# Column tiles for a decoder stage's products, maxima rows sent by GpSimd, and a narrow causal mask

## The reference

```
x = _layernorm(x + _L0_attn_ref(...))    # a0: 8 heads of 32, band of +-64 keys, then a GELU FFN
x = _layernorm(x + _L0_xattn_ref(...))   # x0: 16 heads of 16, keys from ctx, causal mask
x = _layernorm(x + _L0_ffn_ref(...))     # FFN with LoRA experts
x = _layernorm(x + _L1_attn_ref(...))    # a1: 16 heads of 16, full attention
x = _layernorm(x + _L1_xattn_ref(...))   # x1: 16 heads of 16, keys from ctx, full with key mask
x = _layernorm(x + _L1_ffn_ref(...))     # top 2 of 8 experts
```

## Time and profile before

| | us |
|---|---|
| median of 3 runs (lowest, highest) | 3195.89 (3194.34, 3197.38) |
| the profiled execution | 3194.37 |
| its span | 3192.6 |
| mean granted TensorE clock | 0.937 of 2.4 GHz |

### The profile page before, as it was taken

One profiled execution on the slowest core, in us unless ns is written; L12 is line 12 of the kernel. 1 busy time (PEld: TensorE's weight loads), 2 busy tenths in 40 slices (PEclk: granted clock), 3 DMA queues, 4 the chain that ended last, 5 costly groups with the idle time before them and its releaser, 6 DMA issues. The chain is left out here.

```text
span 3192.6 us, 83730 instructions
## 1 busy us (share of the span) xinstructions
PE 2810.0 (88%) x34974; PEld 1425.7 (45%) x34975; DVE 2065.5 (65%) x4240; ACT 1568.0 (49%) x2122; POOL 223.8 (7%) x295
## 2 busy tenths in 40 slices
PE   6686987999996997799999999999999999379992
PEld 3474552444544563144434343443433343246661
DVE  3345137888845236688999898988898985312224
ACT  2222322666662322266777776776776768023331
POOL 2001201000000002300000000000000000210003
PEclk9888997999997999699999999999999999589996
DMA  5412033011001004312112212111111110710012
GB/s 155 119 43 94 1 91 91 3 39 39 3 2 37 1 0 126 88 41 64 45 43 51 60 34 55 44 44 54 43 45 44 44 44 2 257 45 31 31 33 87
DMA packets 112871, 173.46 MB, mean 54 GB/s; under 512 B 17882, under 2 KB 88427, under 8 KB 112147
## 3 DMA queue, kind: packets, MB, share of 16 engines
q1 hardware_dynamic: 109460, 160.11, 17.4%
q0 software_dynamic: 3072, 8.39, 0.8%
HBM read 127.63 MB, written 40.51 MB: 53 GB/s over the span
## 5 line engine op out<-in xcount | busy, mean ns | idle before, releaser
L1304 DVE TENSOR_REDUCE d_part_max<-d_ps_m 128x1 f32<-128x512 f32 (+1 forms) x1964 | 1128.0, 631 | 93.5 <-PE d_ps_m L1291 57.0
L1612 ACT ACTIVATE d_prob<-d_ps_s 128x1024 f32<-128x1024 f32 x928 | 898.8, 1021 | 347.8 <-PE d_ps_s L1481 341.0
L1291 PE MATMUL d_ps_m<-k_st,q_st 97*32 97x512 bf16 (+1 forms) x5296 | 482.0, 363 | 19.4 <-DVE d_part_max L1304 15.9
L1481 PE MATMUL d_ps_s<-q_st,k_st 98*32 98x512 bf16 x5104 | 441.8, 383 | 9.8 <-ACT d_prob L1612 8.4
L690 DVE TENSOR_REDUCE x_part_max<-x_att_ps_m 128x1 f32<-128x512 f32 (+2 forms) x578 | 309.4, 586 | 50.4 <-PE x_att_ps_m L675 22.7
L936 ACT ACTIVATE x_att_prob<-x_att_ps_s 128x1024 f32<-128x1024 f32 (+3 forms) x296 | 258.7, 921 | 140.7 <-PE x_att_ps_s L817 84.6
L1499 PE MATMUL d_ps_o<-d_prob,a_values 128*32 128x512 f32 x2048 | 267.7, 596 | 0.0
L1291 PEld LDWEIGHTS d_ps_m<-k_st,q_st 97*32 97x32 bf16 x5296 | 142.9, 96 | 273.5 <-DVE d_part_max L1304 128.0
L1291 PE MATMUL d_ps_m<-q_st 97*32 97x512 bf16 (+1 forms) x2560 | 232.1, 361 | 2.3 <-DVE d_part_max L1304 0.4
L1481 PEld LDWEIGHTS d_ps_s<-q_st,k_st 98*32 98x32 bf16 x5104 | 138.5, 97 | 195.2 <-issue 83.2
L1499 PE MATMUL d_ps_o<-d_prob,x_values 128*32 128x512 f32 x1664 | 215.5, 593 | 0.4 <-ACT d_prob L1612 0.4
(11 more groups left out here) (326 smaller groups left out, 3329.1 us busy)
## 6 DMA issues: line engine op xcount, KB each, us to landing
k_st<-parts_k SPq DMA_DIRECT2D x90, 256.0 KB, 5.6
k_st<-parts_k SPq DMA_DIRECT2D x90, 208.0 KB, 4.3
l_w<-in_l_w SPq DMA_DIRECT2D x16, 1024.0 KB, 11.7
q_st<-parts_q SPq DMA_DIRECT2D x48, 256.0 KB, 4.7
q_st<-parts_q SPq DMA_DIRECT2D x192, 64.0 KB
q_st<-parts_k SPq DMA_DIRECT2D x30, 256.0 KB
q_st<-parts_k SPq DMA_DIRECT2D x30, 208.0 KB
parts_q<-a_proj_parts SPq DMA_DIRECT2D x16, 384.0 KB, 2.5
```

Source lines behind the costliest of these rows:

```text
L1291: mm = pe.matmul(bank[q:q + COLUMNS, 0:w], self.query(s, h, ROW_MASK + 1, a * P + q, COLUMNS), self.key(s, h, ROW_MASK + 1, k, w), start=T ...
L1304: dve.tensor_reduce(self.part[:, h * QT + a, i:i + 1], bank[:, 0:w], AX.X, ALU.max).then_inc(s_read, 1)
L1481: mm = pe.matmul(ps_s[u][k:k + COLUMNS, hh, :], maxima.key(s, h, ROW_MAX + 1, kt * P + k, COLUMNS), maxima.query(s, h, ROW_MAX + 1, 0, QC) ...
L1612: act.activation(prob[:, p % 2, 2 * u:2 * u + 2, :], ps_s[u][:, :, :], ACT.Exp, scale=scale).then_inc(s_prob, 1)
```

## The change

Three parts. The products of `out_product`, `unit_product` and `v_product` are issued as four column tiles of 32 output partitions; the transposes stay as they are. In `attend` GpSimd sends the rows of maxima instead of SyncE, behind its copy of the group's values, in a written-out loop; rows found during the projection are still sent by SyncE, on a semaphore of their own, and SyncE now waits for the last value product before what follows the stage (in a0 the clearing of the expert slots). The causal mask of the maxima products is 128 columns wide and is added to the last 128 columns of the block alone.

```diff
-    c["causal_q"] = sb("causal_q", [P, QC], BF16)
+    c["causal_q"] = sb("causal_q", [P, P], BF16)
...
     def send(self, sp, x, s_read):
-        self.maxima.send(sp, 0, self.turn_at[x], s_read, x + 1)
+        self.maxima.send(sp, self.maxima.s_early, 0, self.turn_at[x], s_read, x + 1)
...
+    def sent(self, engine, n):
+
+        if type(n) is int and n < self.early:
+            engine.wait_ge(self.s_early, 16 * self.at.heads * (n + 1))
+        else:
+            engine.wait_ge(self.s_sent, 16 * self.at.heads * (n + 1 - self.early))
...
             else:
-                m = cst["causal_q"][:, QC - w:QC]
+                m, edge = cst["causal_q"][:, :], bank[:, w - P:w]
             for q in range(0, P, COLUMNS):
-                mm = pe.matmul(out[q:q + COLUMNS, :], cst["ident_bf"][:, q:q + COLUMNS], m, start=False, stop=True,
+                mm = pe.matmul(edge[q:q + COLUMNS, :], cst["ident_bf"][:, q:q + COLUMNS], m, start=False, stop=True,
                                skip_group_check=True)
...
         @block.sync
         def _(sp):
-            def group(g, stream, last):
-                if not last:
-                    sp.wait_ge(s_load, 16 * LOADS * (g + 1))
-                    sp.wait_ge(s_pv, 2 + pairs_before(g, 0))
-                    load_stacks(sp, at, g + 1, slot(g + 1), q_st, k_st, parts_q, parts_k, s_load)
-                for (dg, c), x in stream.turn_at.items():
-                    maxima.send(sp, slot(g + dg), c, s_mred, entries_before(g) + x + 1)
-
             load_closing(sp, *closing)
             with sp.Fori(0, NG - 1) as g:
-                group(g, body, False)
-            group(NG - 1, end, True)
+                sp.wait_ge(s_load, 16 * LOADS * (g + 1))
+                sp.wait_ge(s_pv, 2 + pairs_before(g, 0))
+                load_stacks(sp, at, g + 1, slot(g + 1), q_st, k_st, parts_q, parts_k, s_load)
+            sp.wait_ge(s_pv, 2 + pairs_before(NG, 0))
             behind(sp)
...
-            def group(g):
+            def group(g, stream):
                 pool.wait_ge(s_pv, 2 + pairs_before(g, 0))
                 for some in (slice(0, V_FIRST), slice(V_FIRST, at.tiles)):
                     pool.tensor_copy(v_grp[:, some, :, 0:SH],
                                      v_tok[:, some, bass.ds(g * GH * SH, GH * SH)]
                                      .rearrange("p t (j d) -> p t j d", d=SH)).then_inc(s_vgrp, 1)
-
-            with pool.Fori(0, NG - 1) as g:
-                group(g)
-            group(NG - 1)
+                for (dg, c), x in stream.turn_at.items():
+                    maxima.send(pool, maxima.s_sent, slot(g + dg), c, s_mred, entries_before(g) + x + 1)
+
+            for g in range(NG):
+                group(g, body if g < NG - 1 else end)
...
                 for m in range(DT):
-                    mm = pe.matmul(plan.bank(step)[:, 0:D], o_fm[:, n % 2, m, :],
-                                   wo_sb[:, plan.chunks[k][0], m, :], start=(m == 0), stop=(m == DT - 1))
+                    for q in range(0, P, COLUMNS):
+                        mm = pe.matmul(plan.bank(step)[q:q + COLUMNS, 0:D], o_fm[:, n % 2, m, q:q + COLUMNS],
+                                       wo_sb[:, plan.chunks[k][0], m, :], start=(m == 0), stop=(m == DT - 1),
+                                       skip_group_check=True)
                 mm.then_inc(s_prod, 1)
```

More of the change, by code:

```diff
@@ L185, in _ @@
             fill(c["eps"][:, :], EPS)
-            off = QC - P
             fill(c["causal_k"][:, :], 0.0)
@@ L189, in _ @@
             fill(c["causal_q"][:, :], 0.0)
-            select(c["causal_q"][:, :], ALU.is_ge, NEG, off, [[-1, QC]], 1)
+            select(c["causal_q"][:, :], ALU.is_ge, NEG, 0, [[-1, P]], 1)
             fill(c["band_k"][:, :, :], 0.0)
@@ L643, in __init__ @@
         self.row = sb(f"{name}_neg_row", [self.columns, P], BF16)
+        self.early = len(MaxStream.windows(at)[0].turn_at)
         self.s_found = nc.alloc_semaphore(f"{name}_neg")
+        self.s_early = nc.alloc_semaphore(f"{name}_early")
         self.s_sent = nc.alloc_semaphore(f"{name}_negd")
-        cst["semaphores"] += [self.s_found, self.s_sent]
+        cst["semaphores"] += [self.s_found, self.s_early, self.s_sent]
+    def sent(self, engine, n):
[3 more added lines that the diff above has]
+            engine.wait_ge(self.s_sent, 16 * self.at.heads * (n + 1 - self.early))
     def product(self, pe, g, entry, bank, s_product):
@@ L670, in product @@
             if at.kind == "band":
-                m = cst["band_q"][:, k - t * P + BAND:k - t * P + BAND + w]
+                m, edge = cst["band_q"][:, k - t * P + BAND:k - t * P + BAND + w], out
             else:
-                m = cst["causal_q"][:, QC - w:QC]
+                m, edge = cst["causal_q"][:, :], bank[:, w - P:w]
             for q in range(0, P, COLUMNS):
-                mm = pe.matmul(out[q:q + COLUMNS, :], cst["ident_bf"][:, q:q + COLUMNS], m, start=False, stop=True,
+                mm = pe.matmul(edge[q:q + COLUMNS, :], cst["ident_bf"][:, q:q + COLUMNS], m, start=False, stop=True,
                                skip_group_check=True)
@@ L685, in reduce @@
             if not (type(n) is int and n == 0):
-                dve.wait_ge(self.s_sent, 16 * self.at.heads * n)
+                self.sent(dve, n - 1)
             dve.tensor_copy(self.row[:, :], bank[:, :].bitcast(BF16)[0:self.columns, 0:P]).then_inc(s_read, 1)
@@ L695, in reduce, with send @@
             dve.wait_ge(self.s_found, n + 1)
-    def send(self, sp, slot, c, s_read, count):
-        sp.wait_ge(s_read, count)
+    def send(self, queue, s_sent, slot, c, s_read, count):
+        queue.wait_ge(s_read, count)
         for h in range(self.at.heads):
-            sp.dma_start(self.q_st[ROW_MAX:ROW_MAX + 1, bass.ds(slot, 1), self.at.halves * h,
+            queue.dma_start(self.q_st[ROW_MAX:ROW_MAX + 1, bass.ds(slot, 1), self.at.halves * h,
                                    c * QC:(c + 1) * QC],
-                         self.row[h * QT:(h + 1) * QT, :]).then_inc(self.s_sent, 16)
+                         self.row[h * QT:(h + 1) * QT, :]).then_inc(s_sent, 16)
 def attend(nc, at, name, v_tok, parts_q, parts_k, o_tok, stacks, maxima, s_load, closing, cst, behind):
@@ L879, in group @@
                     n = g * NQ + c
-                    pe.wait_ge(maxima.s_sent, 16 * HEADS * (n + 1))
+                    maxima.sent(pe, n)
                     for i, kt in enumerate(at.key_tiles(c)):
@@ L1557, in unit_product @@
                 for d in range(DT):
-                    mm = pe.matmul(plan.bank(step)[:, 0:n], w_sb[:, 0 if side == "q" else 1, d, m * P:(m + 1) * P],
-                                   src[:, d, k:k + n], start=(d == 0), stop=(d == DT - 1))
+                    for q in range(0, P, COLUMNS):
+                        start = m * P + q
+                        mm = pe.matmul(plan.bank(step)[q:q + COLUMNS, 0:n],
+                                       w_sb[:, 0 if side == "q" else 1, d, start:start + COLUMNS],
+                                       src[:, d, k:k + n], start=(d == 0), stop=(d == DT - 1), skip_group_check=True)
                 mm.then_inc(s_mm, 1)
@@ L1566, in v_product @@
                 for d in range(DT):
-                    mm = pe.matmul(plan.bank(step)[:, 0:D], ctx_sb[:, d, i * P:(i + 1) * P], w_sb[:, 2, d, :],
-                                   start=(d == 0), stop=(d == DT - 1))
+                    for q in range(0, P, COLUMNS):
+                        start = i * P + q
+                        mm = pe.matmul(plan.bank(step)[q:q + COLUMNS, 0:D], ctx_sb[:, d, start:start + COLUMNS],
+                                       w_sb[:, 2, d, :], start=(d == 0), stop=(d == DT - 1), skip_group_check=True)
                 mm.then_inc(s_vmm, 1)
```

## The result

The changed kernel takes 3159.51 us (median of 4 runs, 3158.04 to 3163.09) against 3196.14 us for the kernel before in the same series: ratio 0.9887, 95% interval 0.987 to 0.9905. That is 36.6 us less; 25.6 were forecast. The time lies inside the forecast range of 3154 to 3187, and the gain was 11 us larger than the forecast. The profiled execution took 3158.21 us, span 3156.4, granted clock 0.938 (0.937 before).

What follows compares the result with a forecast made beforehand. TensorE, busy 88% of the span, was taken to bound the kernel. Terms -17.8 (a0), +7.2 (x0 sends), -8 (mask) and -7 (products) sum to -25.6 us: from 3195.9 to 3170 us, range 3154 to 3187.

Steps and rivals of the forecast that it cites:

- a0, rows: Band stage a0: GpSimd sends remove the 35.6 us wait for rows, but loads are late next; -17.8 us in sum.
- the second wait: a0, entry 21 of the maxima stream: TensorE waits for loads, about 5.7 us in two groups, 2.6 in the first.
- the low clock: a0: the two long new idle times lower TensorE's clock again, 2.2 us for each, +4.4 us.
- x0, sends: Causal stage x0: four GpSimd sends bring chunk 3's row 1.8 us later in each of four groups, +7.2 us.
- my lower bound, as SyncE: x0: the lower bound for the sends' cost, 0, if GpSimd's sends take as long as SyncE's.
- Mask: x0: mask products shrink from up to 512 columns to 128; -8 us, bounds -3 and -12.4.
- Products: Decoder stage: column tiles save 25 round trips of draining the array at 0.32 us; -7 us, bounds 0 and -8.
- slower tiles: Decoder stage: column tiles are slower than whole products, their gain lost or worse; 3177 or 3194 us, 3%.
- The row travels with the loads: a0: the row lands only when the loads are through, so a0 gives nothing; 3188 us, 5%.
- No second wait: a0: loads come sooner than thought, 35.6 us and about 6 of low clock gained; 3147 us, 4%.
- VectorE binds: x0 and decoder: VectorE is the limit, so masks and products give nothing; 3185 us, 9%.
- dear sends: a0 and x0: GpSimd's sends cost much more than priced; at 3.5 us extra 35 us are lost, 3205 us, 5%.

Runs made afterwards that it cites:

- e6_due: The changed kernel with x0's planner wanting each row of maxima two pairs ahead of its chunk instead of one and a half; 3155.56 us, ratio 0.9881.
- e1: The kernel before with only the rows of maxima sent by GpSimd, mask and products as before; ratio 0.9933.
- e2_mask: The kernel before with only the narrow causal mask, sends and products as before; ratio 0.9969.
- e3: The kernel before with only the decoder's output, projection and value products in four column tiles; ratio 0.9978.
- e5_load_early: The changed kernel with SyncE starting the next group's twelve loads after the last scores of the group before, not its last value product; ratio 0.9909.
- e9_paced: The changed kernel with loads started after the previous group's last scores, at most three of twelve on their way; 3148.29 us, ratio 0.9865.

## Why the prediction was right, and where it was off

The time fell inside the range, 5.5 us above its low end, and the two largest mechanisms, a0 and the tiled products, are as forecast. That it stayed inside is owed to the width of the range and in part to luck: the other errors all went towards more gain, x0's sends by their sign and the mask by 1 us, and the 5 us of the experts' stage hadn't been reasoned at all.

- **a0, rows.** Right in mechanism and nearly in size: -15.8 for -17.8, -15.8 to -19.4 over four traces. The waits for the row fell to 3.7 (3 to 8 forecast), the second wait came at entry 21 with 6.8 and 5.8 us (5.7 each), the low clock with 2 and 2.5 us. Group 1 gave less than said: its row was 3.7 us late and 2.9 us of standstill followed, for one wait of 2.6. That is the contention with the loads, which I had at 1.5 us and which is 4 there (7.4 us from copy to use against 3.4, the shortest of a0, in its last group). In e6_due, with the same a0, that row was 2.6 us late and 1.1 us of standstill followed, so this group varies from execution to execution.
- **x0, sends.** Wrong. The step that failed is "I take GpSimd's spacing, as it is the same engine": the spacing was that of indirect gathers, 1.26 us, and a plain send takes 0.51. Not even my lower bound, as SyncE, reached it: +7.2 was forecast, and measured were -3.2 with the wide mask (e1) and -0.1 to -2.4 with the narrow one. The wait of the scores for the row was to grow from 6.5 to about 14 us and stayed at 6.4. Some 7 to 10 of the 11 us are here. The bound "as SyncE" left out that the other engine may be cheaper.
- **Mask.** -8 forecast, -9.0 measured. The savings of 105 and 56 ns for the widths between are right, though the earlier trace rows doesn't show them: the trace has 326 ns for 384 columns and 277 for 256. e2_mask shows the split in the second group: from the start of chunk 3 to the next group 34.45 us for 36.30 (7.4 us in four groups; 6.6 forecast), and up to chunk 3 67.63 for 68.21 (2.3 in four; 3.0 less 1.5 forecast). Both parts were a little larger. The row waits of x0 grew from 6.5 to 7.7 us in e2_mask, near the 1.5 us that were taken off. Over all kernels with SyncE's sends x0 took 408.1 to 409.5 us with the wide mask and 399.9 and 401.2 with the narrow one, a gain of 6.9 to 9.6.
- **Products.** -7 forecast, -7.0 (e3) and -7.6 measured. The gap that a value product leaves beyond its own time is gone, 0.31 us (0.32). The rival of slower tiles is out: 0.87 us for 0.86. The Trainium skill's figure of 2.38 for three tiles (*TensorE: Matmul & The Clock Gate*, Part 3) would, by the prediction's estimate for four, have made these products 16.6 us longer; the trace doesn't agree.
- **Experts.** -5.0, put at nothing in the prediction, and still without a cause; another 4.7 us between x0 and the decoder stage were lost and 3 gained in stages that vary by that much.
- **The rivals.** *The row travels with the loads*, given 5%, didn't happen in groups 2 and 3 of the change, where the loads start late, and cost 3.7 us in group 1; e5_load_early shows that it is real: no packet of the row starts before 144.5, almost 7 us after its copy ended. *No second wait*, *VectorE binds* and *dear sends* are out by the rows above.

## What to carry to other kernels

A wait is worth what the next wait behind it leaves: before counting on 35.6 us, find the next thing that the same loads hold up. A small transfer on the critical path should be sent before bulk loads are queued, or the loads be issued only a few at a time (three of 256 KB here, which ended no later than twelve at once); another issuing engine alone doesn't get it past them. And a price taken from another kind of instruction on the right engine is no price: the row of the same kind on another engine was nearer.

## What the runs showed of the hardware that was not expected

- GpSimd issues a plain send in 0.51 us, less than SyncE with 0.73, and the data of four sends of 1 KB is used 3.46 us after the copy in three of four groups (4.31 in one), against 4.12 in three and 3.62 in one by SyncE.
- A row of 2 KB in all was used 12.0 us after its copy behind eleven issued loads of 256 KB from another engine, with its first packet after 144.5, more than 5 us behind the end of its issue, and 5.5 us when at most three loads were on their way. The Trainium skill has the engines take turns between queues by packet (*DMA: Bandwidth & Descriptors*, "Queues, rings and completion order"). By that rule alone the row would not wait for most of another queue's bytes as it does here. The same page, under "Issuing engines are not separate DMA queues", says that transfers of all issuing engines run on the same 16 DMA engines and that issuing from several saves only issue time; e5_load_early agrees, as the row was issued by 139.14 and came late all the same.
- TensorE stood still for 5.44 us without a releaser while those loads ran, and for 0.98 once they were paced. The profile's page lists a queue of instruction transfers: 266 of them in the five kernels that leave TensorE's products whole, 272 in the nine with products in column tiles. e3_tiles changes TensorE's program alone and has 272, so this queue carries TensorE's instructions, among others perhaps. While the loads ran unpaced none of its packets started between 138.0 and 144.5 us, and two did in the same stretch of e9_paced. So TensorE waiting for its own instructions behind the loads fits well; no trace names it as the releaser, and it isn't shown.
- The experts' stage is some 4.5 us of 324 shorter in every kernel in which GpSimd has sent rows in a stage that ended over 1800 us earlier, and in no other. The cause is open.
